# A perceiver stack of six layers on one core: keys and values of a second cross attention formed twelve batches earlier, with the solve, the filter taps and both expert layers reordered

## The reference

```
x += xattn0(LN(x), ctx, mask)   # 1 head: softmax(q k^T / 16) v, out projection, layer norm
x += delta(LN(x))               # chunks of 32: solve (I + A) per head, two FIR filters over v
                                # (3 and 31 taps), gates from a fused MLP, RMS norm, out projection
x += moe0(LN(x))                # 8 experts, top 2, 1024 hidden, SiLU
x += xattn1(LN(x), ctx)         # 16 heads of 16: k = ctx Wk + bk, v = ctx Wv + bv
x += attn(LN(x))                # 16 query heads, 4 key heads, rotary
x += moe1(LN(x))                # 16 experts of 128, top 4, and 4 shared pieces of 128, relu^2
```

## Time and profile before

| what | value |
|---|---|
| three runs | 1839.52, 1840.7, 1841.96 us (median 1840.7) |
| profiled execution | 1847.41 us, its span 1845.6 us |
| mean granted clock of PE | 0.932 |
| busy: PE, DVE, ACT, POOL | 1607.3, 1165.7, 797.8, 623.5 us |

### The profile page before, as it was taken

One profiled execution on the slowest core, in us unless ns is written; L12 is line 12 of the kernel. 1 busy time (PEld: TensorE's weight loads), 2 busy tenths in 40 slices (PEclk: granted clock), 3 DMA queues, 4 the chain that ended last, 5 costly groups with the idle time before them and its releaser, 6 DMA issues. The chain is left out here.

```text
span 1845.6 us, 41140 instructions
## 1 busy us (share of the span) xinstructions
PE 1607.3 (87%) x16490; PEld 1228.2 (67%) x16490; DVE 1165.7 (63%) x2401; ACT 797.8 (43%) x1871; POOL 623.5 (34%) x495
## 2 busy tenths in 40 slices
PE   6886969899987959999998498999989688879998
PEld 3443447555575659999997364566668578578897
DVE  4567579862068347667661326677769777647887
ACT  1223652121143423444442235788828522536665
POOL 2330000000020067777743304687638544102210
PEclk9987989999899969999999798999989879989999
DMA  9891039612031555655638762555400000001001
GB/s 281 291 293 54 18 112 202 129 47 41 0 120 65 171 205 180 218 195 207 205 110 187 190 217 78 182 164 163 130 24 1 14 21 10 12 6 36 23 7 47
DMA packets 143212, 214.84 MB, mean 116 GB/s; under 512 B 38128, under 2 KB 116528, under 8 KB 137136
## 3 DMA queue, kind: packets, MB, share of 16 engines
q1 hardware_dynamic: 106848, 104.06, 19.2%
q0 software_dynamic: 10368, 58.47, 9.6%
q10 hardware_dynamic: 25808, 49.68, 9.2%
HBM read 164.91 MB, written 47.25 MB: 115 GB/s over the span
## 5 line engine op out<-in xcount | busy, mean ns | idle before, releaser
L286 PE MATMUL ps<-kv_ctx,kv_w 128*128 128x257 f32 x512 | 136.7, 404 | 45.3 <-PEq L1800 18.6
L1488 POOL TENSOR_TENSOR b0m_pm<-b_dr,b_gates 128x256 f32<-128x256 f32 x16 | 13.2, 828 | 408.6 <-SPq L1453 382.2
L1976 DVE TENSOR_TENSOR f_hL<-f_hr,f_hH 128x512 fp32r<-128x512 f32 x92 | 85.0, 961 | 100.1 <-ACT f_hH L1927 100.1
L2134 POOL TENSOR_TENSOR a_pr<-a_pr,a_inv 128x1028 f32<-128x1028 f32 x64 | 121.6, 1900 | 71.8 <-DVE a_inv L2254 71.5
L286 PEld LDWEIGHTS ps<-kv_ctx,kv_w 128*128 128x128 f32 x512 | 96.8, 200 | 67.9 <-issue 33.2
L290 PE MATMUL ps<-kv_w,kv_ctx 128*128 128x256 f32 x512 | 127.9, 394 | 15.7 <-ACT b_kv L310 11.3
L96 PE MATMUL ps<-f_xTH,f_w1H 128*128 128x256 f32 x368 | 107.7, 293 | 24.2 <-issue 23.6
L290 PEld LDWEIGHTS ps<-kv_w,kv_ctx 128*128 128x128 f32 x512 | 97.3, 196 | 34.1 <-ACT b_kv L310 13.0
L2224 ACT ACTIVATE a_pr<-ps,a_neg 128x257 f32<-128x257 f32 x256 | 117.7, 477 | 2.6 <-DVE a_neg L2274 2.6
L97 PE MATMUL ps<-f_xTL,f_w1H 128*128 128x256 f32 x368 | 105.8, 287 | 0.0
L98 PE MATMUL ps<-f_xTH,f_w1L 128*128 128x256 f32 x368 | 105.7, 287 | 0.0
(11 more groups left out here) (419 smaller groups left out, 4598.3 us busy)
## 6 DMA issues: line engine op xcount, KB each, us to landing
a_kv<-kv SPq DMA_DIRECT2D x64, 513.0 KB, 3.6
a_ctxT<-in_ctxT SPq DMA_DIRECT2D x32, 514.0 KB, 6.9
a_ctxR<-in_ctx SPq DMA_DIRECT2D x32, 512.0 KB
kv<-b_kv ACTq DMA_DIRECT2D x31, 513.0 KB, 5.6
kv_ctx<-in_ctxT ACTq DMA_DIRECT2D x61, 257.0 KB
kv<-f_raw ACTq DMA_DIRECT2D x15, 513.0 KB
outs<-f_yo SPq DMA_DIRECT2D x23, 256.0 KB
kv<-f0r_kv ACTq DMA_DIRECT2D x9, 513.0 KB, 6.3
```

The costliest lines, as they stand in the source:

```text
L286: done = e.matmul(out[:, 0:NK], self.w[:, 0, c, cols(part)], ctx[:, c, :], start=(c == 0), stop=(c == DC - 1))
L1976: e.tensor_tensor(h[1][:, j % 2, 2 * q:2 * q + 2, :], hr[:, q, :, :], h[0][:, j % 2, 2 * q:2 * q + 2, :].bitcast(F32), ALU.subtract).then_ ...
L2134: e.tensor_tensor(pr[:, b % 3, :, :], pr[:, b % 3, :, :], inv[:, b % 2, :].unsqueeze(2).to_broadcast([P, HG, NK]), ALU.mult).then_inc(*p_p ...
```

## The change

`AHEAD` becomes `(12, 24, 7, 15, 6)` for a0, b0, f0r, f0 and a1q. The twelve batches of a0 are the first batches of tiles 2 to 13; their context is taken from the `ctxT` ring of a0 itself, so that they load none. The ring grows to `KS` = 4, and a slot is loaded again only when the parts of its tile are formed. `A.begin` (Wk, Wv, bk) moves up on SP's queue behind tile 1, and the three first contexts of the other batches (`A.contexts`) stay at its end. b0s hosts 21 parts fewer, f0r 6 and a1q 9. In b0s four taps go with each `taken` instead of three, the first solve has none beside it, and the last 26 steps of the second have one instead of two; `fuse_most(0)` is the first of PE's work there, and `fuse_most(2)` comes behind `half_outputs(1)`. In f0 the casts for `w1` of the next block come before those for `w2` of this one, on POOL and on DVE. In g the ring of `h` grows from 8 to 12, outputs follow their hidden part by `LEAD` = 7 jobs instead of 2, the shared outputs are made a tile at a time behind each hidden part (7 to 22), and DVE's ranking is cut in pieces between them.

```diff
-AHEAD = (31, 9, 15, 9)
+AHEAD = (12, 24, 7, 15, 6)
+NEAR = range(2, 2 + AHEAD[0])
...
+        own = [BT * t for t in NEAR]
+        self.order = own + [b for b in range(B) if b not in own]
...
-            b, part = divmod(j, 3)
-            s, many = b % self.SLOTS, len(self.banks)
-            ctx, out = self.ctx[s], self.K.ps[:, self.banks[(j - self.first) % many], :]
+            i, part = divmod(j, 3)
+            s, many = self.slot(i), len(self.banks)
+            ctx, out = self.near.get(i, self.ctx[s]), self.K.ps[:, self.banks[(j - self.first) % many], :]
...
                 e.wait_ge(*self.ev.at(j + 1))
-                e.dma_start(self.K.kv[b], kv).then_inc(*self.st[s].up(16))
+                e.dma_start(self.K.kv[self.order[i]], kv).then_inc(*self.st[s].up(16))
...
-    KS, GT = 3, 4
+    KS, GT = 4, 4
...
+        A.host(Y, AHEAD[0], (6, 7), places(sb("kv", [P, 2, KV])))
+        A.near = {i: ctxT[:, t % KS, :, 0, :] for i, t in enumerate(NEAR)}
...
+                    if t - KS in NEAR:
+                        e.wait_ge(*A.mm.at(3 * (t - KS - NEAR[0]) + 3))
...
+                    if t == 1:
+                        A.begin(e)
                 K.front.load(e)
-                K.keys.begin(e)
+                A.contexts(e)
...
                     if tile(t - 1):
                         turn_probs(t - 1)
+                    if t in NEAR:
+                        if t == NEAR[0]:
+                            e.wait_ge(*v_w.at(4))
+                        A.pe(e, 2)
...
                         outputs(t - 4)
+                    if t in NEAR:
+                        A.pe(e, 1)
...
                     if t % GT == GT - 1 and tile(t + 1):
+                        if t in NEAR:
+                            A.wait_taken(e)
                         queries((t + 1) // GT)
...
+                    if t in NEAR:
+                        A.act(e, 2)
                     if tile(t):
                         exponents(t)
                     if tile(t - 2):
                         mixed(t - 2)
+                    if t in NEAR:
+                        A.act(e, 1)
...
-                ahead.pe(e, 18)
                 fuse_most(0)
-                ahead.pe(e, 8)
+                ahead.pe(e, 3)
                 ahead.wait_taken(e)
                 half_outputs(0)
...
-                ahead.pe(e, 4)
-                fuse_most(2)
+                ahead.pe(e, 6)
                 ahead.wait_taken(e)
                 half_outputs(1)
+                fuse_most(2)
                 fuse_rest(2)
...
                     taken(t)
-                    fir_taps(3)
-                solve(0, L - 1, 1, 1)
+                    fir_taps(4)
+                solve(0, L - 1, 1, 0)
                 solve(1, L - 1, 27, 2)
                 for t in range(H2):
                     outputs(t)
-                solve(1, 26, 1, 2)
+                solve(1, 26, 1, 1)
...
-                    high2(j)
                     if j + 1 < BLOCKS:
                         high1(j + 1)
+                    high2(j)
...
-                    low2(j)
                     if j + 1 < BLOCKS:
                         low1(j + 1)
+                    low2(j)
...
-    E, SH, WS, HS, RING = F.EXPERTS, F.SHARED, F.SLOTS, 8, 8
+    E, SH, WS, HS, RING = F.EXPERTS, F.SHARED, F.SLOTS, 12, 8
+    LEAD = 7
...
-                shared(0)
-                hidden(7)
-                for n in range(8, len(jobs) + 2):
+                for n in range(LEAD, len(jobs) + LEAD):
                     if n < len(jobs):
                         hidden(n)
-                    if n in (8, 12, 16):
-                        shared(n // SH - 1)
-                    if n >= SJ + 2:
-                        outputs(n - 2)
+                    if n < LEAD + SJ:
+                        shared(*divmod(n - LEAD, 4))
+                    else:
+                        outputs(n - LEAD)
...
-                for n in range(12, len(jobs) + 2):
+                for n in range(LEAD, len(jobs) + LEAD):
                     if n < len(jobs):
                         low(n)
-                    if n in (13, 17):
-                        shared(n // 4 - 1)
-                    if n >= SJ + 2:
-                        outputs(n - 2)
+                    if n >= LEAD + SJ:
+                        outputs(n - LEAD)
+                    elif n % 2:
+                        shared(*divmod((n - LEAD) // 2, 2))
+                    ranks(n - LEAD)
```

More of the change, by code:

```diff
@@ L253, in __init__ @@
         self.formed = self.taken = self.first = self.last = 0
+        own = [BT * t for t in NEAR]
+        self.order = own + [b for b in range(B) if b not in own]
+        self.near = {}
     def host(self, Y, count, banks, kv):
@@ L259, in host, with slot, load @@
         self.st = [Y.sig("dma", f"kv{s}") for s in range(len(kv))]
-    def load(self, e, b):
-        s = b % self.SLOTS
-        e.dma_start(self.ctx[s], self.K.ins["ctxT"][b, :, :].rearrange("(c p) k -> p c k", p=P)).then_inc(*self.ld_c[s].up(16))
+    def slot(self, i):
+        return (i - len(NEAR)) % self.SLOTS
+    def load(self, e, i):
+        s = self.slot(i)
+        e.dma_start(self.ctx[s], self.K.ins["ctxT"][self.order[i], :, :].rearrange("(c p) k -> p c k", p=P)).then_inc(*self.ld_c[s].up(16))
     def begin(self, e):
@@ L268, in begin, with contexts @@
         e.dma_start(self.bk[:, :], self.K.ins["L1_xattn_bk"]).then_inc(*self.ld_w.up(16))
-        for b in range(self.SLOTS):
-            self.load(e, b)
+    def contexts(self, e):
+        for i in range(self.SLOTS):
+            self.load(e, len(NEAR) + i)
     def pe(self, e, n):
         for j in range(self.formed, min(self.formed + n, self.last)):
-            b, part = divmod(j, 3)
-            s, many = b % self.SLOTS, len(self.banks)
-            ctx, out = self.ctx[s], self.K.ps[:, self.banks[(j - self.first) % many], :]
+            i, part = divmod(j, 3)
+            s, many = self.slot(i), len(self.banks)
+            ctx, out = self.near.get(i, self.ctx[s]), self.K.ps[:, self.banks[(j - self.first) % many], :]
             if j == 0:
                 e.wait_ge(*self.ld_w.at(48))
-            if part == 0:
-                e.wait_ge(*self.ld_c[s].at(16 * (b // self.SLOTS + 1)))
+            if part == 0 and i not in self.near:
+                e.wait_ge(*self.ld_c[s].at(16 * ((i - len(NEAR)) // self.SLOTS + 1)))
             if j - self.first >= many:
@@ L301, in act @@
         for j in range(self.taken, min(self.taken + n, self.last)):
-            b, part = divmod(j, 3)
-            own = b - self.first // 3
+            i, part = divmod(j, 3)
+            own = i - self.first // 3
             s = own % len(self.kv)
@@ L838, in _ @@
                 K.norms["b0"].act(e)
+                A.end(e)
 H0, DV0 = 4, 64
@@ L1301, in _ @@
                     ahead.act(e, 1)
-                ahead.act(e, 54)
+                ahead.act(e, 31)
                 e.wait_ge(*ld_2.at(96))
@@ L1307, in _ @@
                     if g == 2:
-                        ahead.act(e, 4)
+                        ahead.act(e, 6)
                         for t in range(H2, NT):
@@ L2944, in hidden, with shared @@
                     done.then_inc(*t_h.up())
-                def shared(g):
+                def shared(g, tile):
+                    half, t = divmod(tile, 2)
                     for x in range(SH):
                         e.wait_ge(*v_l.at(SH * g + x + 1))
[L2949 to L2955, removed]
+                    if g and t == 0:
+                        e.wait_ge(*v_y.at(2 * g + half - 1))
+                    for x in range(SH):
+                        done = product3(e, K.ps[:, 4 + half, cols(t, D)], [q[:, (SH * g + x) % HS, cols(tile)] for q in h],
+                                        [w[:, x, D:2 * D] for w in w1], x == 0, x == SH - 1)
+                    if t:
                         done.then_inc(*t_y.up())
@@ L3041, in low, with shared, ranks @@
                     e.tensor_tensor(h[1][:, n % HS, :], hr[:, n % 2, :], h[0][:, n % HS, :].bitcast(F32), ALU.subtract).then_inc(*v_l.up())
-                def shared(g):
-                    for half in range(2):
-                        e.wait_ge(*t_y.at(2 * g + half + 1))
-                        row = 4 * g + 2 * half
-                        e.tensor_tensor(K.x[:, row:row + 2, :], K.x[:, row:row + 2, :],
-                                        K.ps[:, 4 + half, :].rearrange("p (t d) -> p t d", d=D), ALU.add).then_inc(*v_y.up())
+                def shared(g, half):
+                    e.wait_ge(*t_y.at(2 * g + half + 1))
+                    row = 4 * g + 2 * half
+                    e.tensor_tensor(K.x[:, row:row + 2, :], K.x[:, row:row + 2, :],
+                                    K.ps[:, 4 + half, :].rearrange("p (t d) -> p t d", d=D), ALU.add).then_inc(*v_y.up())
+                def ranks(n):
+                    if n == 0:
+                        R.R_e.compare(e, 0)
+                    if n == 1:
```

(9 more changed lines are left out.)

37 lines of the change are left out of this document (12 added, 25 removed).

## The result

Six runs of the changed kernel took 1812.88 to 1831.85 us, 1822.16 in the median, against 1840.95 for six of the kernel before (1837.79 to 1845.76): ratio 0.9899, interval [0.9863, 0.9936]. The change makes the kernel 1.0% faster, 18.8 us; forecast were 37.7 us and a range of 1786 to 1823. The median lies at the edge of the range, and the gain is just under half of the forecast.

The account below looks back on a forecast made before the run. The prediction took PE, busy 87% of the span, to bound the kernel, so only its idle time could be won. Its terms, 24 - 15 + 1 - 18 - 10.7 - 19 = -37.7 us, gave 1803 us, range 1786 to 1823.

Parts of the forecast that it names:

- a0, +24: In a0, twelve more batches make a tile 9.6 us on PE, with transfers passing under it: +24 us (+18 to +34).
- Rival (a): Transfers, not PE, set a0, at 12.3 us a tile: +32 there, 1835 us in all; chance 12%.
- b0s, -15: In b0s, 21 parts fewer and the new order leave DVE's chain as the bound: -15 us (-7 to -22).
- a1q, -10.7: In a1q, nine parts go that stood with nothing else on PE to do: -10.7 us.
- f0r, +1: In f0r, six parts fewer win nothing, since PE idles waiting for DVE instead: +1 us (0 to +3).
- f0, -18: In f0, swapped casts end `low1` 2.2 us earlier, so PE's stop in each block vanishes: -18 us (at most -20).
- experts_1, -19: In experts_1, the longer distance and one shared tile at a time remove most of PE's stops: -19 us (-16 to -22).
- The rule weighed: Skill's rule for a0: the share of weight loads shows how full PE is, 44%, so it takes most batches in stride.
- rival (d): PE has room in a0, a tile taking its transfers' 8.5 us: +10 instead of +24, 1789 us; chance 5%.

Follow-up runs that it names:

- experiment 6: The changed kernel without a0's twelve stores of keys and values, SP writing the weight buffer in their place at the end of its b0s queue: 1823.43 us, ratio 0.9963.
- experiment 8: The kernel before with f0's swap, gather2 behind the casts and the new experts_1, no batch in a0, b0s in its old order: 1782.79 us, ratio 0.9746.
- Experiments 1 and 2: The changed kernel with f0's casts in the old order: 1831.69 us, 0.9955; the kernel before with the swap of f0's casts alone: 1835.23 us, 0.9972.
- experiment 3: The changed kernel with POOL's gather2 of the next block behind the block's two casts instead of ahead of them: 1803.93 us, ratio 0.9809.
- the second series: Runs on the second chip, where the changed kernel was run again beside the kernel before: 1805.71 us, ratio 0.987.

## Why the prediction was wrong

- **a0, +24:** right, in mechanism and nearly in size. The tile is 8.30 us, and four tiles with their queries take 39.4, 9.84 each (from the starts 59.71 and 99.08), against 9.6 forecast; tiles 2 to 13 took 116.2 us, against 115. The last tile's context was late by 0 to 6.2 us in the six profiles of the twelve batches, and a0 cost 22 to 31 us. The transfers, 276 to 284 GB/s between 60 and 130 us, stay barely ahead of PE, slower than the 318 that the prediction took. Rival (a) did not happen: without its stores a0 won only 1.8 us (experiment 6).
- **b0s, -15:** 18.2 on the first chip, 9.5 on the second, 18.8 on the third. The second differs by its old b0, mostly through the granted clock behind the second outputs (experiment 8). DVE is the bound after, as forecast: its chain reached `half_outputs(0)` at 377.4 in a layer that starts 27.7 us later, and PE waited 10.5 us before the first outputs and 8.4 before the second (the prediction's sums give 13.7 and 7):

```profile
377.37 1.93 PE L1244 MATMUL ps<-b_dr,b0s_AS 32*32 32x64 f32 x64 [10.47 <-issue]
...
441.44 1.93 PE L1244 MATMUL ps<-b_dr,b0s_AS 32*32 32x64 f32 x64 [8.35 <-issue]
```

- **a1q, -10.7:** to the tenth.
- **f0r, +1:** +2.9 here, -0.7 to +3.0 elsewhere; within its bounds but for one.
- **f0, -18: this step failed.** "Swapped, `low1` ends 2.2 us earlier and the stop vanishes." I took the lateness of the gather as a cost to POOL alone, and weighed it against POOL's spare time. What it moved is the casts. They began 2.0 us behind PE's first product of the block before (802.73 against 800.76) and 4.6 us behind it after (800.59 against 796.02), and so fell whole onto the one stretch in which DVE forms `f_hL`; DVE did none of these while POOL cast. DVE and POOL then run as a ring, each waiting for the other: both subtractions (4.4 us), 0.35 to the gather, 2.2 us to the casts, both casts (3.7), the four `f_hL` behind them (2.3), which add up to the block's 12.97 us within 0.02. Before, the same work was in the same ring. The gather, let go by `low2`, then ran beside `low1` and took 2.75 us instead of 0.94, to 0.8 us behind the end of `low1`, so the casts waited for both subtractions all the same: they began 2.1 us behind the second one before and 2.5 us after. The swap changed the order within the ring and not its length. Experiments 1 and 2 show the step to be worth 5.3 to 6.0 us of the blocks, at their ends, and experiment 3 that another 17.7 us come when the casts no longer wait for `low2`. No run takes the casts off POOL; that the wait of `f_hL` for them closes the ring is read from the timelines. The kernel before showed it already, in a row that I had not read by itself: its first `f_hL` of a block took 1.96 us, its last 0.68.
- **experts_1, -19:** -19.2 in the profile, -17 by itself.
- **The moves together** (a0, b0s with its order, f0r, a1q) were forecast at -0.7 us and came to +1.9 in the two profiles: what the forecast hoped to win lay in f0 and experts_1.
- With f0's term corrected, the forecast would have been 37.7 - 12.5 = 25.2 us, at the edge of the interval (11.8 to 25.2 us) and near the 24.2 of the second series. The other misses in the profiles nearly cancel (a0 +3.9, b0 -3.2, f0r +1.9). The 6.4 us that are left to 18.8 are within the scatter of the six runs (1812.88 to 1831.85), and no series splits them.
- **The rule weighed,** that PE has room where weight loads are few: wrong here. a0 grew by 27.9 us for 42.8 us of added work, since only 16.4 of its 109 us had been idle; rival (d) had +10. The row was right.

## What to carry to other kernels

When an edit delays work on an engine, ask what runs elsewhere at the new time, not only whether the engine has time to spare: here DVE could not subtract two tensors of SBUF while POOL cast one. Work moved into idle time is free only up to that idle time: three batches in a0 cost nothing, twelve cost 22 to 31 us there, at most the price of the nine others (32 us). And an order tuned for one load, as b0s's, can be a loss under another, so order and load are tried together.

## What the runs showed of the hardware

DVE's subtraction of two SBUF tensors and POOL's cast in SBUF exclude each other, and the loser waits for the whole instruction, or for two in a row: `f_hL`, 0.68 us alone, took 1.96 us against the rest of one cast, 1.75 at the end of another and 4.56 against two, and ended 0.55 to 0.56 us behind the cast each time. POOL loses in the same way: its gather of weights took 0.94 us by itself and 2.75 in 21 of the 23 blocks of the kernel before, where it ran beside `low1`, and ended 0.81 to 0.82 us behind it. The Trainium skill (SBUF — State Buffer, SBUF: two separate sides) states it: the second port pair of DVE is POOL's only one, whoever comes first holds it for the whole instruction, and a DVE operation with two SBUF inputs contends for it with a POOL instruction that reads SBUF. The casts and `f_hL` agree with that rule. It would have told the prediction to place the casts against `f_hL` and not against POOL's spare time.

The series differed in the rate of their transfers: for the stretch from the last block of f0 to a1q 205 to 215 GB/s on the first chip, 224 to 239 on the second and 201 to 215 on the third, and the kernel before is 11 us faster on the second. That stretch took 102 to 107 us there against 113 to 119 on the other two. Each chip ran one series only, so whether the chip or the hour made the difference is not shown.
